# A row normalisation's product, made by VectorE instead of GpSimd in the second node phase of a four-layer graph kernel

## What is computed

```python
def _gcn_layer(x, src, dst, ew, Ws, bs, Wn, bn, bias):
    msg = x[src] * ew[:, None]
    agg = segment_sum(msg, dst) + x
    cnt = segment_sum(ones_like(ew), dst) + 1.0
    neigh = agg / cnt[:, None]
    out = x @ Ws.T + bs + neigh @ Wn.T + bn + bias
    return where(out > 0, out, 0.2 * out)

def _L0(x):
    h = x
    for l in range(2):
        h = _gcn_layer(h, ..., W_self[l], b_self[l], W_neigh[l], b_neigh[l], layer_bias[l])
    return h @ W_agg.T + b_agg

def _layernorm(x, eps=1e-05):
    m = mean(x, axis=-1); v = var(x, axis=-1)
    return (x - m) / sqrt(v + eps)

x = _layernorm(x + _L0(x))        # end of the first layer; three more layers follow
```

## Time and profile before

| what | us |
|---|---|
| median of 3 runs | 4401.65 |
| lowest and highest of them | 4396.96, 4405.56 |
| span of the profiled execution | 4783.9 |
| that execution's own time | not on the page; the span, from the first to the last instruction, is what there is |
| phase `d1` in that span | about 1603 to 2001 |

### The profile page before, as it was taken

The page is one execution under the profiler, slowest core; times in us unless marked ns, Lnnn a source line. Parts: engine busy times, 40 slices in busy tenths (PEclk is TensorE's granted clock), DMA queues, the critical chain, the costliest instruction groups (busy, mean ns, idle before and its releaser), DMA issues.

```text
span 4783.9 us, 90087 instructions
## 1 busy us (share of the span) xinstructions
PE 3733.3 (78%) x18662; PEld 2281.7 (48%) x18662; DVE 3413.8 (71%) x13249; ACT 2211.2 (46%) x4608; POOL 2954.6 (62%) x3411
## 2 busy tenths in 40 slices
PE   2155799998778999777899999995678774778776
PEld 1012344477523455422598888894224442234443
DVE  5338965355665577743498988897877888768898
ACT  0000046733225688633366666664145652256666
POOL 4650355366566699866466666664665776656787
PEclk6556899999889999889899999997899997999999
DMA  3340157777524788534555555552456773467776
GB/s 88 99 74 6 53 173 222 251 230 232 168 86 159 246 259 271 175 124 130 170 166 161 167 162 161 161 168 66 122 180 227 235 234 113 147 194 246 226 238 194
DMA packets 536159, 810.98 MB, mean 170 GB/s; under 512 B 129245, under 2 KB 184005, under 8 KB 535709
## 3 DMA queue, kind: packets, MB, share of 16 engines
q1 hardware_dynamic: 318844, 532.13, 35.3%
q10 hardware_dynamic: 162769, 169.41, 10.5%
q0 software_dynamic: 54096, 104.47, 8.0%
HBM read 493.49 MB, written 311.41 MB: 168 GB/s over the span
## 4 chain that ended last, share of the span: by engine, by line
PE 47%; DVE 19%; issue 14%; DVEq 6%; POOL 6%; DMA 3%; another core or an unknown queue 2%; ACT 1%; POOLq 0%; ACTq 0%; SPq 0%; PEldq 0%
PE ps L1554 18%; DVEq L68 5%; DVE stat L1122 4%; PE ps L1719 4%; PE ps L1700 4%; PE ps L1701 4%; DVE hit L1071 3%; PE ps L1487 3%; POOL got L719 2%; PE ps L1679 2%; POOL x2T L734 2%; PE ps L1710 2%; PE ps L1680 2%; DVE mv L1128 2%
## 5 line engine op out<-in xcount | busy, mean ns | idle before, releaser
L754 POOL TENSOR_TENSOR rstd<-vare,neg_half 128x4 f32<-128x4 f32 x686 | 710.3, 1035 | 430.6 <-DVE vare L1135 429.6
L1554 PE MATMUL ps<-hit,got 128*128 128x512 bf16 x1172 | 492.5, 420 | 381.7 <-issue 155.9
L1316 ACT ACTIVATE evac<-ps 128x512 f32<-128x512 f32 x392 | 233.4, 595 | 861.8 <-PE ps L1554 625.3
L719 POOL DMA_INDIRECT got<-nodes_l,sorted_by_dst x392 | 398.2, 1016 | 239.5 <-PE ps L1554 109.8
L1554 PE MATMUL ps<-hit,tail 128*128 128x512 bf16 x1172 | 490.2, 418 | 22.8 <-issue 20.8
L1554 PE MATMUL ps<-hit,rest 128*128 128x512 bf16 x1172 | 491.9, 420 | 20.2 <-issue 18.9
L1163 DVE TENSOR_TENSOR nT<-sums,ps 128x512 f32<-128x512 f32 x392 | 268.9, 686 | 270.8 <-PE ps L1599 100.3
L1301 ACT ACTIVATE ps<-zeros 128x512 f32<-128x512 f32 x588 | 344.3, 598 | 195.0 <-DVEq L428 170.1
L1554 PEld LDWEIGHTS ps<-hit,got 128*128 x1172 | 121.8, 104 | 649.3 <-issue 566.0
L719 POOL DMA_INDIRECT got_pair<-in_x,sorted_by_dst x196 | 203.5, 1038 | 363.5 <-DVEq L428 190.1
L669 POOL DMA_INDIRECT records_by_src<-record,place_src x196 | 201.1, 1026 | 162.0 <-PE ps L1587 90.6
(11 more groups left out here) (276 smaller groups left out, 10298.4 us busy)
## 6 DMA issues: line engine op xcount, KB each, us to landing
nodes_l<-xout SPq DMA_DIRECT2D x196, 256.0 KB
xin<-nodes_l SPq DMA_DIRECT2D x196, 256.0 KB
sums<-sums_l SPq DMA_DIRECT2D x196, 256.0 KB
sums_l0a<-evac_pair ACTq DMA_DIRECT2D x98, 256.0 KB
sums_l<-evac_pair ACTq DMA_DIRECT2D x98, 256.0 KB
sums<-sums_l0a SPq DMA_DIRECT2D x98, 256.0 KB
sums_l0b<-evac ACTq DMA_DIRECT2D x98, 256.0 KB
sums<-sums_l0b SPq DMA_DIRECT2D x98, 256.0 KB
```

The costliest lines, as they stand in the source:

```text
L719: pool.indirect_dma_start(out=BUFFERS[name].got[0][:, k % RING, :], out_offset=None, in_=table, in_offset=bass.IndirectOffsetOnAxis(ap=sor ...
L754: pool.tensor_tensor(rstd[:, n, at, :], vare[:, n, at, :], neg_half[:, :], ALU.pow)\
L1316: act.activation(w.evac[h][:, slot, :], ps[:, BANKS * h + g % BANKS, :], ACT.Copy).then_inc(s["out"].sem, 1)
L1554: last = pe.matmul(into, part.rearrange("p a d -> p (a d)"), w.hit[:, i % w.hits, :], start=False, stop=False, skip_group_check=True)
```

## The change

`power` gets an argument with which it makes the root alone. In phase `d1` POOL uses it so, and no longer signals `rstd`. DVE gets a stage `shifts` with lag 13, three turns after the residual (lag 10) and two after the moments (lag 11) of the same group: it waits for the root, makes shift and signals `rstd`, for which ACT waits as before. In a turn it stands between the residual and the drain ahead of the row statistics. At the end of the phase POOL waits for `root0` instead of `rstd`.

```diff
-            def power(phase, n, ready, done):
+            def power(phase, n, ready, done, shifted=True):
...
                     pool.tensor_tensor(rstd[:, n, at, :], vare[:, n, at, :], neg_half[:, :], ALU.pow)\
                         .then_inc(s[f"root{n}"].sem, 1)
+                    if not shifted:
+                        return
                     held(*s[f"root{n}"](i + 1))
                     pool.tensor_tensor(shift[:, n, at, :], negmean[:, n, at, :], rstd[:, n, at, :], ALU.mult)\
                         .then_inc(s[done].sem, 1)
...
-            beside("d1", ("add", "x2", "rstd"), lambda: pipeline(pool, GROUPS, 8, [(add_x, 4), (join, 8), (power("d1", 0, "var", "rstd"), 12)]))
+            beside("d1", ("add", "x2", "root0"), lambda: pipeline(pool, GROUPS, 8, [(add_x, 4), (join, 8), (power("d1", 0, "var", None, False), 12)]))
...
-                pipeline(dve, GROUPS, 8, [(average(s, 0, "add"), 5), (residual, 10)] + row_stats((10, 0, res, s["var"])))
+                def shifts(i, q, slot):
+                    dve.wait_ge(*s["root0"](i + 1))
+                    at = slot % 4
+                    dve.tensor_tensor(shift[:, 0, at, :], negmean[:, 0, at, :], rstd[:, 0, at, :], ALU.mult).then_inc(s["rstd"].sem, 1)
+
+                pipeline(dve, GROUPS, 8, [(average(s, 0, "add"), 5), (residual, 10), (shifts, 13)] + row_stats((10, 0, res, s["var"])))
```

## The result

| | before | after |
|---|---|---|
| median of 5 runs, us | 4401.65 | 4372.39 |
| lowest and highest | 4396.96, 4409.83 | 4370.67, 4378.53 |
| ratio, with its 95% interval | | 0.9935 [0.9924, 0.9946] |

The trace of before shown above (span 4783.9 us) comes from a chip on which the whole program takes about 4780 us, and so do the experiments e, f and g. The runs in the table, the trace of after and the experiments h come from chips on which it takes about 4400. So an experiment is compared with the runs of before on its own chip, by their ratio, printed with its 95% interval; h2, h3 and e1 are one run each and have none.

A forecast was written before the change was run, and what follows sets the result against it. POOL was taken to bound 78 turns of the second node phase, then PE: 78 x 3.687 = 287.6 us plus 8.7 for loop ends is 296.3 against 310.9, 14.6 less, so 4401.65 becomes 4387 us; range 4375 to 4404.

The forecast's parts named there:

- POOL, one instruction and one wait less: Phase d1: POOL's turn falls to 3.52 us, PE at 3.687 becomes the bound, 0.30 us a turn can reach the time.
- VectorE's product, 0.16 us: Phase d1: one more 128x4 tensor_tensor a turn on VectorE, 0.16 us, hidden by 0.82 us of idle time before nT.
- What can hold it, 0 to 1.27 us, taken as 0.6: Phase d1: VectorE's new product may wait for POOL's running add or join, 0 to 1.27 us, middle 0.6.
- The wait for the root: Phase d1: the root is there 0.28 us before VectorE's product needs it; costed at nothing.
- VectorE's loop ends, 2.2 us each, 8.7 together: Phase d1: with PE as bound, VectorE's pauses at four loop ends cost PE 2.2 us each, 8.7 in all.
- The first 15 turns, the last four: Both ends of phase d1: the first 15 turns don't change; the last four give 0 to -2 us, taken as 0.
- The phase shorter by 14 to 15 us, everything else shifted.: Sign to look for: the phase from 1603 us on shorter by 14 to 15 us, all else only shifted.
- The carry from the profiled span to the runs: Whole program: the 14.6 us from the profiled span carried to the runs' median in us, not as a share.
- A: Rival, d1: POOL and VectorE in step at 3.82 us a turn, only 4 us gained, 4398 us; chance 0.14.
- B: Rival, d1: unprofiled POOL turns already near PE's, only slack removed, -1 to -5 us, 4399 us; chance 0.14.
- C: Rival, d1: the product stops the statistics behind POOL's join, 4.88 us a turn, slower, 4425 us; chance 0.09.
- D: Rival, d1: VectorE's loop-end pause shrinks or is no part of a run, -23 us, 4378 us; chance 0.09.

The follow-up runs named there:

- h2: Kernel before with 65 idle instructions behind VectorE's program of d1, which move d3a's loop; one run, 4398.86 us, d3a 319.3.
- h3: Kernel before with 113 idle instructions behind VectorE's program of d1, which move d3a's loop; one run, 4414.22 us, d3a 336.9.
- e1: Kernel before, unchanged, profiled once more; one run, 4771.98 us, 93 turns of d1 366.5 us.
- e2: Changed kernel in which POOL also waits for its root and makes a product that nobody reads; ratio to before 0.9981, 93 turns 368.2 us.
- h1: Changed kernel with 48 idle instructions behind VectorE's d0 and 80 behind its d1; ratio to before 0.9929, 93 turns 341.98 us.
- e3: Changed kernel with d1's product left out on both engines, ScalarE taking negmean as bias; ratio to before 1.0017, 93 turns 371.6 us.
- h4: Changed kernel without d1's product, VectorE's d1 loop cut to 8 turns, 25 idle instructions behind it; ratio to before 0.9959, 93 turns 347.6 us.
- f2: Kernel before with 40 idle instructions at the end of VectorE's d1; ratio to before 0.9974, d1 399.2 us, d3a 318.7, d3b 454.6.
- f3: Changed kernel with 90 idle instructions at the end of VectorE's d1, later code back at before's place modulo 128; ratio to before 0.9968, d3a 333.5 us.
- f1: Changed kernel, unchanged, run again on the chip of the other experiments; 93 turns of d1 348.3 us, d3a 318.3.
- g2: Changed kernel without d1's product, with a VectorE memset of 128x4 in its place; ratio to before 0.9958, 93 turns 356.8 us.
- g4: Changed kernel with the node phases written out on every engine, no hardware loops there; 4666.59 us beside 4781.24 for before.

## Why the prediction was right, and where it failed

*POOL, one instruction and one wait less.* Right. Power to add is 0.99 us, in the 0.98 to 1.10 given; PE became the bound at 3.687; POOL's gap before the add is ended by ScalarE's xT, 0.26 us. Undisturbed, its turn is 3.45 us (1552.53 to 1555.98), the lower end of the 3.45 to 3.57 given. e2, where the product on POOL takes d1's gain away, shows where it came from.

*VectorE's product, 0.16 us.* 98 rows, min, median and max 127, 153 and 816 ns. ScalarE waited for it 45.6 us in 72 of its turns. Costed at nothing, this wait did reach POOL's add, 1.4 us at each loop end; it didn't reach PE, which in h1 kept 3.687 us with the same product. These are the answer for the tile shift:

```profile
L1198 DVE TENSOR_TENSOR shift<-negmean,rstd x98: 127/153/816, 1388.6 to 1738.9; 128x4 f32<-128x4 f32 x98
...
  DVE shift L1198: 45.6, 72
```

*What can hold it, 0 to 1.27 us, taken as 0.6.* The mechanism is there, and for the product the middle was far too high: one of its 98 rows is over 0.2 us. In that case it took 0.82 us and ended as POOL's add did (1513.73 and 1513.71), DVE first, then POOL:

```profile
1512.91 0.82 DVE L1198 TENSOR_TENSOR shift<-negmean,rstd 128x4 f32<-128x4 f32 x1
...
1512.44 1.27 POOL L727 TENSOR_TENSOR sums<-sums,xT 128x512 f32<-128x512 f32 x1
```

The prediction drew on the Trainium skill (SBUF — State Buffer, Who interferes with whom), where the later of two such instructions blocks until the first has finished. This pair agrees; but the rule says only what happens when the two meet, and the product rarely met one. negmean, queued behind it, met one in nearly every turn: 0.3 to 0.4 us at PE's pace and about 0.77 while VectorE caught up behind a loop end, for 0.15, ending as POOL's add did (1506.59 and 1506.56 in after). The slack hid it here; e3 and h4 show its price where the two are in step.

*The wait for the root.* Right: no stand for it but 1.2 us in all, in two turns.

*VectorE's loop ends, 2.2 us each, 8.7 together.* The step is right, its size half too large (8.7 for 5.9). PE's turns with a loss were 4.96, 5.76, 4.51 and 5.39 us: 5.9 us over 3.687. The slack was right (forecast 2.25; 3.37 late at turn 32, 1.27 of it lost, so 2.10). The lateness was oversized: 4.4 us forecast, 3.5 on average, as I took the longer of two stands and added a hold of 0.6 that did not come.

*The first 15 turns, the last four.* 55.30 us, as said. PE's four turns behind the 94th took 9.96 us for 10.57, and the last normalisation ended 1.4 us later behind the 94th turn than in before: about nothing in all, as taken. From the 16th to the 94th turn PE alone takes not 287.6 but 286.7 us (h1: 341.98 less 55.30). With 5.8 for loop ends that is 292.5, the measured 347.80 less 55.30: **d1's own step is 18.4 us where 14.6 was forecast.** The difference is the stall term, 2.9, and 0.9.

*"The phase shorter by 14 to 15 us, everything else shifted."* **This is the step that failed.** The change adds 39 instructions to VectorE's program, 17 of them in the body of the loop of d1, and all later code of that engine lies 39 further on. In before d3a's loop lay where its four ends each fetch code; 39 on it doesn't. That is 15 to 16 us gained there and 5 to 6 lost in d3b, where the loop (486 instructions) stands at either place; what makes d3b longer was not looked for. f2 gets both with no other change, and f3 takes them away and leaves 15 us. The prediction had a term for neither: it carried the saving in d1 over to the whole as if later stages could only shift. That the total lies outside the range comes from this and from d1's 3.8 us more. The trace of before had it in sight, in a timeline row of DVE at turn 32 of d3a:

```profile
3753.88 0.69 DVE L1163 TENSOR_TENSOR nT<-sums,ps 128x512 f32<-128x512 f32 x1 [3.80 <-issue]
```

A stand as long as those of d1, released by nothing that the profile shows. I priced the ones in d1 and didn't ask what decides whether there is one.

*The carry from the profiled span to the runs.* It held. Clock and edge stages differ by chip, but PE's 93 turns do not: 347.80 us here and 348.3 in f1.

*The rivals.* A, in step, did not come, but e3, g2 and h4 show it as it was described, with a turn of 3.77 (worked out: 3.82). B, that runs have no such gain, falls with f3. C, the product stopping the statistics behind the join, did not come. D, that VectorE's stand shrinks with its changed code, did not come in d1, where the stands are 3.4 to 4.3 us still; in d3a just that happened, which nobody had asked.

## What to carry to other kernels

A loop with a long body can stand at each of its ends while code is fetched, 3 to 6 us on VectorE here for bodies of 309 to 762 instructions, and whether one of 310 or 326 does so hangs on where it lies. The stand doesn't show in the time while another engine is the bound. Before costing a change that adds instructions, look at what later loops of the same engine do at their ends, and compare traces stage by stage: a few instructions of no cost can move one by 15 us. And take engines that get into each other's way as a pair: what matters is whether their turns lock, and a change as small as one instruction less can bring that about.

## What the runs showed of the chip that I had not expected

- VectorE's loop of 326 instructions stands at its ends or not by where it lies: 48 idle instructions ahead of it take the stands away (h1: 341.98 us for 93 turns against 347.80), with 8 packets of code in 300 us for 29. A period of 128 instructions and a limit of three blocks fit its loops of d1, d3a and d3b in every kernel here that has them, with one fitted constant; a loop of another engine was not moved.
- With an instruction of 0.15 us left out, 93 turns of d1 took 23 us longer (e3: 371.6 against 348.3 in f1), since VectorE's negmean then waits 1.0 us behind GpSimd's join in nearly every turn, and GpSimd's power waits 0.27 for it. What starts the lock, the missing product or a pause of 0.44 us at one place of the loop, is open.
- Writing out the loops of all node phases gave 2.5% (g4), though VectorE's program alone grew from 9416 to 16354 instructions by it.
- One kernel takes 4400 us on some chips and 4780 on others. The difference lies in the setup (376 against 523 us), four of the five edge stages and d0, not in the phases that PE or POOL fills.
